# Loading the first operands of a fused kernel as fp32 through two hardware queues, with the rounding to bf16 done on chip

## What is computed

```python
def _rfs(xw, ab, AB, gs):                    # random features
    dot_products = jnp.einsum('...d,rd->...r', xw, ab[:, None] * gs)
    correction = (0.5 * jnp.sum(xw * xw, axis=-1))[..., None] * (ab * ab)
    return 1.0 / math.sqrt(NUM_RFS) * AB * jnp.exp(dot_products - correction)

weights = _rfs(input_weights, ab, AB, proj_matrix)       # ab = xis, AB = exp(xis)
feats = _rfs(x, ab, AB, proj_matrix)
attn = jnp.einsum('bsr,or->bso', feats, weights)
x = _layernorm(x + attn)
h = silu(x @ wg.T) * (x @ wu.T)                          # int8 weights / 127, 3072 wide
x = _layernorm(x + h @ wd.T)
```

## Time and profile before

| | us |
|---|---|
| median of 3 runs (633.03 to 634.0) | 633.85 |
| the profiled execution | 632.33 |
| its span, core 0, first to last instruction | 630.4 |
| spans of the 8 cores | 626.8 to 630.4 |
| busy on core 0: TensorE matmul | 595.7 (95%) |
| VectorE / ScalarE / GpSimd | 429.3 / 197.3 / 372.5 |
| first matmul on core 0 | 9.55 |

### The profile page before, as it was taken

The page is one execution under the profiler, slowest core; times in us unless marked ns, Lnnn a source line. Parts: engine busy times, 40 slices in busy tenths (PEclk is TensorE's granted clock), DMA queues, the critical chain, the costliest instruction groups (busy, mean ns, idle before and its releaser), DMA issues.

```text
span 630.4 us, 9271 instructions; the slowest of 8 cores (626.8 to 630.4 us)
## 1 busy us (share of the span) xinstructions
PE 595.7 (95%) x2776; PEld 272.0 (43%) x2832; DVE 429.3 (68%) x683; ACT 197.3 (31%) x368; POOL 372.5 (59%) x337
## 2 busy tenths in 40 slices
PE   3799999999979899999999999999999999999994
PEld 1244444455534344444444444444444444444441
DVE  1275933555867887777778777777777757886675
ACT  0244424466664222322322232232230013310243
POOL 9201999400002246999999998999813596614940
PEclk9999999999979999999999999999999999999998
DMA  8999261565410011133234224134431829875433
GB/s 99 162 168 268 97 224 35 194 206 191 146 51 0 2 67 68 35 126 121 78 120 154 72 94 154 53 112 137 162 129 56 312 101 307 294 248 184 170 134 135
DMA packets 28193, 86.07 MB, mean 137 GB/s; under 512 B 2416, under 2 KB 9584, under 8 KB 24816
## 3 DMA queue, kind: packets, MB, share of 16 engines
q1 hardware_dynamic: 19696, 54.54, 25.0%
q0 software_dynamic: 8448, 30.94, 19.3%
HBM read 60.82 MB, written 23.59 MB: 134 GB/s over the span
## 4 chain that ended last, share of the span: by engine, by line
PE 81%; DVE 5%; ACT 5%; issue 5%; DMA 3%; POOL 1%; DVEq 0%; ACTq 0%; POOLq 0%
PE P L530 45%; PE P L791 22%; PE P L294 8%; PE P L326 4%; DVE z L456 3%; DMA proj<-projT 3%; ACT junk L427 2%; PE P L258 1%; ACT lnst L428 1%; PE P L359 1%; PE P L438 1%; ACT lnst L430 0%; DVE xsum L185 0%; POOL xf L80 0%; DVE zh L736 0%
## 5 line engine op out<-in xcount | busy, mean ns | idle before, releaser
L530 PE MATMUL P<-x1t,ring 128*128 128x512 bf16 x751 | 181.9, 382 | 5.7 <-ACT ebuf L545 3.9
L185 POOL TENSOR_TENSOR ring<-ring 128x512 bf16<-128x512 bf16 x120 | 135.3, 1161 | 13.2 <-DMA ring<-wgu 9.4
L530 PE MATMUL P<-xsum,ring 128*128 128x512 bf16 x565 | 139.8, 381 | 2.5 <-DVE xsum L185 1.5
L530 PEld LDWEIGHTS P<-x1t,ring 128*128 128x128 bf16 x768 | 75.1, 98 | 96.4 <-issue 7.9
L587 POOL TENSOR_TENSOR hact<-wbuf,hact 128x512 bf16<-128x512 f32 x24 | 27.9, 1161 | 125.6 <-DVE wbuf L584 115.1
L185 POOL TENSOR_TENSOR stage<-stage 128x512 bf16<-128x512 bf16 x60 | 70.8, 1216 | 44.1 <-DMA stage<-wd 42.2
L530 PEld LDWEIGHTS P<-xsum,ring 128*128 128x128 bf16 x576 | 56.4, 98 | 71.0 <-issue 4.5
L791 PE MATMUL P<-tbuf,hact 128*128 128x512 bf16 x376 | 83.3, 379 | 0.4
L294 PE MATMUL P<-xf,proj 128*128 128x512 bf16 x252 | 59.8, 394 | 15.1 <-DMA proj<-projT 13.4
L791 PE MATMUL P<-tbuf,sbuf 128*128 128x512 bf16 x283 | 62.5, 379 | 0.3
L545 ACT ACTIVATE ebuf<-P 128x512 f32<-128x512 f32 x48 | 28.2, 588 | 97.8 <-PE P L530 97.8
(11 more groups left out here) (82 smaller groups left out, 683.0 us busy)
## 6 DMA issues: line engine op xcount, KB each, us to landing
tbuf<-t_hbm SPq DMA_DIRECT2D x14, 1536.0 KB, 8.1
ring<-wgu POOLq DMA_DIRECT2D x12, 1024.0 KB, 5.2
xtok_sb<-xtok SPq DMA_DIRECT2D x16, 512.0 KB, 4.0
t_hbm<-stage SPq DMA_DIRECT2D x8, 896.0 KB, 4.8
stage<-wd POOLq DMA_DIRECT2D x12, 512.0 KB, 3.7
xf<-xfm POOLq DMA_DIRECT2D x16, 256.0 KB, 25.6
x_hbm<-x1k SPq DMA_DIRECT2D x16, 256.0 KB, 2.0
xres<-x_hbm SPq DMA_DIRECT2D x16, 256.0 KB, 6.8
```

Source lines behind the costliest of these rows:

```text
L185: out[o] = (p.mark(eng, lambda e: e.tensor_tensor(view(o), view(i), view(j), op), *toks, *behind),)
L530: fn = lambda e, dk=dk, lhsT=lhsT, rhs=rhs: e.matmul(bank(b), lhsT, rhs, start=(start and dk == 0), stop=(stop and dk == 3), skip_group_ch ...
```

## The change

Three fp32 buffers of 128 x 4096 (`early`, 16 KB in each partition) are laid over areas that are used later: `wt`, the last two tiles of `fe`, and the first slot of `ring`. SyncE issues the four pieces of x tile 0 and then the four of projection group 1; ScalarE issues the four of group 0. VectorE rounds x tile 0 into `xf`, ScalarE the eight pieces of the projection into `proj`. Ahead of its DMAs ScalarE runs an `Exp` on 8 elements in each partition. GpSimd's first load (x tile 1) waits until the second piece of both x tile 0 and group 0 has landed; its 12 loads of those operands are gone.

```diff
+    early = [at(f"early{i}", kb, 4096, F32) for i, kb in enumerate((66, 98, 154))]
...
+    t_zero = p.mark("vector", lambda e: e.memset(lnst[:, 0:8], 0.0))
...
+    t_warm = p.mark("scalar", lambda e: e.activation(lnst[:, 0:8], lnst[:, 0:8], AF.Exp), t_zero)
+
+    def load_early(eng, i, k, src, o):
+        return p.dma(eng, f"ld_early{i}{k}", early[i][:, k * 1024:(k + 1) * 1024], src[:, o:o + 1024])
+
+    ld_early = {}
     for k in range(4):
-        load_x(0, k)
-        load_pj(0, k)
+        ld_early[0, k] = load_early("sync", 0, k, xfm_h, k * 1024)
+        ld_early[1, k] = load_early("scalar", 1, k, projT_h, k * 1024)
+    for k in range(4):
+        ld_early[2, k] = load_early("sync", 2, k, projT_h, 4096 + k * 1024)
+
+    for k in range(4):
+        ld_x[0, k] = p.mark("vector", lambda e, k=k: e.tensor_copy(
+            xf[:, k * 1024:(k + 1) * 1024], early[0][:, k * 1024:(k + 1) * 1024]), ld_early[0, k])
+        ld_pj[0, k] = p.mark("scalar", lambda e, k=k: e.activation(
+            proj[:, k * 1024:(k + 1) * 1024], early[1][:, k * 1024:(k + 1) * 1024], AF.Copy), ld_early[1, k])
+    for k in range(4):
+        ld_pj[1, k] = p.mark("scalar", lambda e, k=k: e.activation(
+            proj[:, 4096 + k * 1024:4096 + (k + 1) * 1024], early[2][:, k * 1024:(k + 1) * 1024], AF.Copy), ld_early[2, k])
     t_ident = p.mark("gpsimd", lambda e: e.affine_select(
         ident[:, :], identsrc[:, :], [[-1, 128]], OP.is_equal, 0.0, base=0, channel_multiplier=1), t_src)
-    for k in range(4):
-        load_pj(1, k)
...
+    p.wait("gpsimd", ld_early[0, 1], ld_early[1, 1])
     for t in (1, 2, 3):
...
     for n in range(2):
-        load_ring(n)
+        load_ring(n, ld_pj[1, 3])
...
-            out, a, AF.Exp, bias=biasx[:, rc:rc + 1], scale=xisc[:, rc:rc + 1]), t_arg, t_bias)
+            out, a, AF.Exp, bias=biasx[:, rc:rc + 1], scale=xisc[:, rc:rc + 1]), t_arg, t_bias, ld_pj[0, 3], ld_x[0, 3])
```

## The result

The changed kernel takes **642.71 us** (median of 5 runs, 642.05 to 644.76) against 633.85 for the kernel before (5 runs): the ratio is **1.0154**, 95% interval 1.014 to 1.0168. That is 8.9 us slower where 2.8 us faster was forecast.

What follows compares the result with a forecast made beforehand. The prediction took TensorE's early wait for the projection's load as the bound: start 3.8, transfer 18.3, tail 1.1, cast 1.06, `sbc` 0.6, handovers 0.15 gave restart 25.0, 2.8 us earlier: 631.0 us, 8-in-10 range 628.3 to 635.2.

Steps and rivals of the forecast that it cites:

- Which queue is served: Assumption that GpSimd's loads, begun when 4 of 12 early pieces have landed, take no bandwidth from the 8 others.
- equal shares: Rival: from about 13.8 us three queues have 113 GB/s each; restart 4.4 us later, 638.2 us; chance 0.12.
- restart: Moment TensorE goes on with unit (0,1)'s fourth matmul, then without gaps; forecast 25.0 us against 27.95 on core 0.
- tail: End of the early transfers, from the full-rate sum to the last piece's landing: 1.1 us, ends 0.5 and 2.
- A smaller share: Rival: GpSimd's stream gets a quarter of the rate; restart 28.0, no change, 633.9 us; chance 0.15.
- more bandwidth: Rival: fp32 copies of the early pieces reach 397 GB/s; restart 22.5, 5.3 us gained, 628.5 us; chance 0.11.
- Start of the transfers: Early loads at kernel start count as at full rate from 3.8 us, between 2.6 and 5.1; first part of the gain.
- Rate: Transfer of the 12 early pieces, 6.29 MB at 343 GB/s: 18.3 us, ends 17.2 and 19.7.
- Table load: ScalarE's 1.28 us of table load leaves the wait for `sbc` and stands at about 2 us, before the first `Exp`.
- ScalarE as the bound: Rival: ScalarE's own group 0 loads come last, five casts and `sbc` follow; restart 28.5, 634.4 us; chance 0.10.
- A microsecond gained at the restart is at least nearly one at the end: Claim from comparing cores: core 1 restarts 2.5 us earlier than core 0 and its span is 3.6 us shorter.
- 4 us to spare: Claim that x tile 1, read by 29.4 to 32 us, is in before unit (1,0) needs its last piece at 36.7.

## Why the prediction was wrong

**The step that failed** is "Which queue is served": "So what was issued first was served first." It rested on one stretch in which GpSimd's packets came late beside SyncE's, and read a lag of the issuer as the order of service. The issue at 90.07 and 8 packets in the window from 92 fit either. The next window speaks against it: SyncE's queue had not "run out" at 93, it got 19 packets beside GpSimd's 94, and 4 more after 94. The runs settle it. In the run that waits for the third pieces, GpSimd's packets don't come in when the engines run empty at 20 us, but only from 21 on, 2.3 us or more after the issue, so the lag is there without a competitor. And where streams overlap, the later one is not held back: three queues get 62, 64 and 59 packets, two get 87 and 88. The Trainium skill ("DMA: Bandwidth & Descriptors", "Queues, rings and completion order") says that each DMA engine takes the queues that have work in turn, packet by packet. The traces agree with it by the counts above, while every queue has plenty of work; whether a packet of the profile is one of that page's, they don't show.

**The rival "equal shares"** (chance 0.12) had the mechanism, and its price of 638.2 was 4.5 short of the median. Its restart of 32.3 against 37.14 on core 3 divides so. At 28 us SyncE's queue had 0.52 MB left; at the 148 GB/s that it had from 24 to 28 they would be in by 31.5, 2.1 us behind the rival's 29.4. That part is start and rate. They took until 35.37 instead: its packets thin out, from 40 in the microsecond from 28 to 12 in that from 33 and 4 in that from 34, while q0 fills what it leaves. This tail of 3.9 us stood in the sum with 1.1, ends 0.5 and 2. The 1.1 was taken from the landing of `xtok`, which had the same competitor: its last 23 packets, a quarter of a microsecond at 100 each, took from 93 to 95.0 beside GpSimd's. The rows give 1.8 rather than 1.1 for that tail. The 2.1 us and the 2.8 by which the tail exceeded 1.1 are the 4.8 within 0.1. The clock and the 0.94 us came on top. *A smaller share* fell the other way: from 18 to 36 us GpSimd wrote 1.73 MB, which is 3.46 read, against 2.25 of the two others, 61% of the reads. Nothing speaks for *more bandwidth*.

**Start of the transfers**, 3.8 with ends 2.6 and 5.1: on core 3 the windows show 64 GB/s from 2 to 4, 119 from 4 to 6 and 283 to 334 from 6 to 12. At 307 GB/s, the mean from 6 to 18, the bytes moved before 6 (0.37 MB) put the start at 4.8, near the upper end. (The rows cited for the ends, 1.46 + 0.9 and 1.46 + 3.4, make 2.4 and 4.9; nothing hangs on the difference.) **Rate**, 343 with ends 320 and 366: 307 as long as only the hardware queues ran, below the lower end of 320. These two terms alone would have used up the gain: with GpSimd held back until all twelve pieces had landed, the restart is at 26.7 to 29.1, against 25.0 forecast and 25.3 to 27.95 before. With 3.8 and 343 the first matmul was forecast at 7 to 9; it came at 11.59 (9.0 to 12.2 over the cores), later than the 9.55 before. So the first part of the gain, an earlier stream, was not there either; the hardware queues are at their rate from 6, as GpSimd's was the earlier trace rows.

**Table load**: right in itself (at 1.43; wait for `sbc` 0.19 where no cast stands in front). **Casts**: 1.06 us on ScalarE as taken; on VectorE 0.69 against 0.81, hidden here, since the restart waits for group 1. **ScalarE as the bound**: its own loads came first, not last, so the rival as put did not occur. But that "ScalarE's list is fixed" was counted with 1.8 us behind the last landing; the early copy of `sbc` shows that the order was worth 0.8% (1.0073 against 1.0154), some 5 us, once the landing was late.

**"A microsecond gained at the restart is at least nearly one at the end"** was wrong for the kernel before. It came from comparing cores whose bytes came earlier altogether: core 1 had both an earlier restart and an earlier x tile 1. The table load alone moved the restart and not x tile 1, and gained nothing. A loss at the restart did count in full, and the clock added to it.

**x tile 1**, "4 us to spare": this took the last piece as needed by unit (1,0)'s own matmuls at 36.7 and left out the correction. The correction of tile 1 starts 53 matmuls behind the restart, at 36.6 by the forecast, and before it come VectorE's second squares and four `arg`, 4.5 us on core 0 before (35.01 to 39.51). The last piece was needed at 32.1, and was forecast for 29.4 to 32: next to nothing to spare. This is the wait that the experiments with an early restart met. In the changed kernel it didn't show: x tile 1 had taken group 1's bandwidth, its squares start at 40.30 without a wait, and its early landing was worth nothing.

## What to carry to other kernels

When a load is moved to another queue, it leaves the order of its old one: queues with work share the engines, so a later stream that is needed later slows the earlier one down from the moment it starts, and only one common queue (or a wait at the right moment) keeps bytes in the order of need. Before a gain is counted at one wait, read the next one: take the landing that follows it, follow it through every engine that works on it, and see how far it is from being waited for. On an engine with a fixed order, an instruction that waits for a DMA belongs behind everything whose inputs are there already.

## What the runs showed of the hardware

- Three queues with work at once got 62, 64 and 59 packets in 2 us (no wait for GpSimd, core 0, 12 to 14), two got 87 and 88 (changed kernel, core 3, 22 to 24). Since GpSimd's packets write about half of what they read, GB/s of a window falls where it joins (295 to 246 from 18:20 to 20:22) though the engines are as busy.
- GpSimd's issue leads its first packets by 2 to 3 us with the engines idle (27.87 to the window from 30; 18.74 to that from 21) and by more than 4 with them busy (13.79 to that from 18). For the single load at 262.57 it was about 1. Why these differ stays open; no run varied it alone.
- A stream that ended beside another had a long thin tail: 0.52 MB took 7.3 us, where 148 GB/s would have taken 3.5. That only some of the 16 engines still had its bytes would explain it, but the profile doesn't part the engines, so this isn't shown.
- The granted clock of core 3 fell to half within an idle stretch of 9.72 us and cost 2.7 us behind it. For short idle stretches their length doesn't tell. Behind the same 2.27 us the clock fell on three cores and cost 1.7, and stayed on five. With GpSimd waiting for all twelve, TensorE stood 2.06 to 3.08 us before the restart, and seven of eight cores kept the full rate (53 in 11.60); core 4, after 3.06, had 0.56 and 0.59 in the windows from 30 to 34 and took 13.29. What decides was not tried. At the very start, matmuls run up to 0.43 us apart though the clock is shown as 1.00 (8 in 3.57 us).
- The same bytes land at different times on different cores: the last cast of group 1 starts at 25.05 to 27.41 with GpSimd held back, at 32.26 to 35.45 in the changed kernel. Whether this comes from the shared memory was not tried.
